# GpSimd held behind each reciprocal root until its normalisation has run, head-group maxima copied as eight rows by two copies, merged comparisons, and another interleaving

## What is computed

```python
x = x + _L0_xattn_ref(_layernorm(x), ctx, ctx, ...)   # 16 heads of 16, softmax
x = x + _L0_ffn_ref(_layernorm(x), gate_w, expert_w)  # x + output of the best of 8 experts
x = x + _L1_xattn_ref(_layernorm(x), ctx, ...)        # 16 heads, scores masked by a fixed pattern
x = x + _L1_ffn_ref(_layernorm(x), ...)               # three cycles of a small gelu net and a twist
x = x + _L2_xattn_ref(_layernorm(x), ctx, ctx, ...)   # linear attention through sigmoids
x = x + _L2_ffn_ref(_layernorm(x), ...)               # linear, plus the best 2 of 8 low-rank experts
x = x + _L3_xattn_ref(_layernorm(x), ctx, ctx, mask, ...)  # one head of 256, softmax
x = x + _L3_ffn_ref(_layernorm(x), ...)               # gated, hidden size 768

def _layernorm(x, axis=-1, eps=1e-05):
    m = jnp.mean(x, axis=axis, keepdims=True)
    v = jnp.var(x, axis=axis, keepdims=True)
    return (x - m) / jnp.sqrt(v + eps)
```

## Time and profile before

| | us |
|---|---|
| three runs | 1043.64, 1046.17, 1047.5 (median 1046.17) |
| profiled execution | 1042.16 |
| its span, first to last instruction | 1040.3 |

### The profile page before, as it was taken

The page is one execution under the profiler, slowest core; times in us unless marked ns, Lnnn a source line. Parts: engine busy times, 40 slices in busy tenths (PEclk is TensorE's granted clock), DMA queues, the critical chain, the costliest instruction groups (busy, mean ns, idle before and its releaser), DMA issues.

```text
span 1040.3 us, 17717 instructions
## 1 busy us (share of the span) xinstructions
PE 973.8 (94%) x6194; PEld 715.1 (69%) x6194; DVE 667.6 (64%) x2250; ACT 561.3 (54%) x1231; POOL 221.8 (21%) x317
## 2 busy tenths in 40 slices
PE   7989889988999999998999999999989999999998
PEld 6765655656577766776587767776577756777777
DVE  5435673577576676777575776774776566746564
ACT  1351645585457653766358643767368543773421
POOL 3004311302240051314030242212221023002210
PEclk9899999999999999999999999999999999999999
DMA  7408525221322031411313211402222004000000
GB/s 234 48 2 237 116 93 111 57 37 32 61 56 62 11 82 32 84 35 35 66 31 68 57 36 26 102 1 55 48 47 51 12 1 101 2 12 1 1 1 21
DMA packets 39927, 56.25 MB, mean 54 GB/s; under 512 B 3968, under 2 KB 35712, under 8 KB 36224
## 3 DMA queue, kind: packets, MB, share of 16 engines
q1 hardware_dynamic: 38448, 46.50, 21.8%
q10 hardware_dynamic: 1392, 8.63, 2.3%
HBM read 39.64 MB, written 13.89 MB: 51 GB/s over the span
## 4 chain that ended last, share of the span: by engine, by line
PE 57%; DVE 16%; ACT 16%; issue 7%; DMA 2%; POOL 2%; SPq 1%; ACTq 0%; DVEq 0%; POOLq 0%
PE bank L1618 7%; PE bank L1945 4%; PE bank L1478 4%; PE bank L1469 4%; PE bank L1675 4%; PE bank L1697 4%; ACT QA L841 4%; PE bank L1956 4%; ACT PT L853 3%; PE bank L1732 3%; PE bank L1590 3%; PE bank L1726 2%; PE bank L1487 2%; ACT L853 2%; PE bank L1678 2%
## 5 line engine op out<-in xcount | busy, mean ns | idle before, releaser
L853 ACT ACTIVATE PT<-bank 128x512 f32<-128x512 f32 x256 | 153.2, 598 | 143.9 <-PE bank L1678 86.6
L1675 PE MATMUL bank<-QA,KA 98*128 98x256 bf16 x512 | 113.2, 273 | 17.2 <-ACT PT L853 15.9
L1618 PE MATMUL bank<-w,xhT 128*128 128x512 f32 x256 | 126.6, 604 | 2.1 <-DVE one L1177 2.1
L1151 DVE CUSTOM_DVE_ANT_0 bank<-bank,maskb 128x256 f32<-128x256 f32 x256 | 102.0, 451 | 26.3 <-PE bank L1590 26.0
L841 ACT COPY QA<-bank 2x256 bf16<-2x256 bf16 x256 | 92.8, 363 | 24.4 <-PE bank L1656 18.4
L1144 DVE TENSOR_REDUCE mx<-bank 128x2 f32<-128x512 f32 x128 | 83.5, 682 | 32.1 <-PE bank L1590 31.4
L1590 PE MATMUL bank<-KA,QA 96*128 96x256 bf16 x512 | 91.0, 274 | 3.2 <-DVE mx L1144 1.4
L1675 PEld LDWEIGHTS bank<-QA,KA 98*128 98x128 bf16 x512 | 46.9, 99 | 64.7 <-issue 43.7
L1945 PE MATMUL bank<-xhBT,wi 128*128 128x256 f32 x336 | 87.6, 391 | 1.4 <-DVE hT L1452 0.6
L1198 DVE SCALAR_TENSOR_TENSOR x<-bank,one,x 128x256 f32<-128x256 f32 x128 | 61.5, 481 | 27.2 <-PE bank L1618 24.7
L1945 PEld LDWEIGHTS bank<-xhBT,wi 128*128 128x128 f32 x336 | 59.6, 192 | 11.5 <-DVE hT L1452 3.2
(11 more groups left out here) (316 smaller groups left out, 2093.1 us busy)
## 6 DMA issues: line engine op xcount, KB each, us to landing
QA<-scratch SPq DMA_DIRECT2D x90, 128.0 KB, 4.4
scratch<-kparts SPq DMA_DIRECT2D x30, 192.0 KB, 2.3
KA<-scratch SPq DMA_DIRECT2D x15, 384.0 KB, 4.6
scratch<-qparts SPq DMA_DIRECT2D x30, 192.0 KB, 2.3
KA<-scratch SPq DMA_DIRECT2D x15, 256.0 KB, 5.4
w<-pack ACTq DMA_DIRECT2D x1, 2409.0 KB, 8.6
wi<-ipack ACTq DMA_DIRECT2D x1, 2304.0 KB, 8.4
xin<-x_in SPq DMA_DIRECT2D x8, 256.0 KB, 5.4
```

Source lines behind the costliest of these rows:

```text
L853: act.activation(PT[:, n % RING, :, :].rearrange("p t s -> p (t s)"), st_bank[:, :], ACT.Exp).then_inc(exp_s, 1)
L1151: last = dve.tensor_tensor_reduce(s, s, maskb[:, t, :], op0=ALU.add, op1=ALU.max, scale=1.0, scalar=-HUGE, accum_out=mx[:, i % 4, n % GH, ...
L1618: last = pe.matmul(bank[n % 2][:, :], xhT[:, kk, t * P:(t + 1) * P], W("exp0", KT)[:, kk, i * 512:(i + 1) * 512], start=(kk == 0), stop=(k ...
L1675: last = pe.matmul(st_bank[:, t * S:(t + 1) * S], KA[m][0:KM, v, t * P:(t + 1) * P], QA[m][0:KM, v, :], start=True, stop=(m == 0))
```

## The change

GpSimd's three root functions end with a wait for the semaphore that VectorE's scaling raises (`xh_s`, or the lane's `xh`), so nothing more runs on GpSimd until that normalisation has run. The maxima of a head group now go to eight adjacent columns of mq, high and low by turns, behind 96 blank ones (MR = 8, KM = 104). The transposed eight rows land on partitions 96 to 103, and every head of the group gets all eight in QA, by one copy for the first head and one for the other three, with the source repeated. KA's eight rows hold ones only in the head's own two: `rows1` makes that pattern from the identity, and `own_rows` spreads it over 16 heads and 256 positions, once for each KA; it waits for the first weights. The second score multiply has 104 rows instead of 98. The pairs of comparisons and of multiplications at L1177, L1358 and L1366 become one `tensor_tensor` each with a repeated second input. The semaphore counts of `negm_s` are adapted. `TURNS` holds the same steps in another order for all five engines, on TensorE with 70 `w` ahead of the first score head, 107 in all, and 64 `z`. On VectorE, `own_rows` stands behind the first sample's scaling and behind its split of the queries (L1064 to 1072), where the two fills had stood first of all. In thread p of the fifth sample (counted from zero), 25 steps of VectorE lie between statistics and scaling in the new order; on GpSimd the split of that sample's keys follows its root.

```diff
--- before.py
+++ after.py
@@ -23,8 +23,9 @@
 
 GROUPS = [(0, 3), (1, 2), (2, 1)]
 KR = PARTS * HD
-KM = KR + 2
-MQ = 32 * (GH - 1) + 2
+MR = 2 * GH
+KM = KR + MR
+MQ = KM
 VW = HD + 1
 E = 8
 R = 4
@@ -87,49 +88,49 @@
...
     "gpsimd":
-        "ppppppssppppsppsssppsppsppasppssspssppaabpppbsbasspbsppaaspppsbppbbsabsppsspppapaspsbbpbsasbsppppspa"
...
+        "ppppppspspppsppssppspppspsasppsspspssappabpbpsbasppbsppsppasasbbpbpsasbsspppppasapbspbpbsabssspppppp"
...
     "tensor":
-        "pwwwppwwwpwwwppwwppwwwwwwwwwwwwwwpwwwwwpwpwwwwwwppwwwwwwwwwwwwwwwwwwwwwwwwwwwsswpsspssvpsvssvsvvswww"
...
+        "pwwwpppwwwppwwwwwwwppwwwwwwwwwwwwwwwwwwwwwwwwwwwwwwpwwwwwpwpwwwwwwppwwwwwwwwwwwwwwwsswpsspssvpssvwsv"
...
@@ -250,6 +251,7 @@
         PT = sb("PT", [P, RING, T, S])
         OT = sb("OT", [P, 2, S])
         rc = sb("rc", [P, T, GH])
+        rows1 = sb("rows1", [KM, GH], BF16)[KR:KM, :]
         att = sb("att", [P, T, D])
         attT = sb("attT", [P, KT, S])
 
@@ -601,11 +603,13 @@
                 pool.wait_ge(stats[t], nth(stats[t], b, n))
                 link(t, pool.tensor_tensor(veps[t][:, :], mv[t][:, :, 1], epsm[:, :], ALU.add))
                 pool.tensor_tensor(rstd[t][:, :], veps[t][:, :], powm[:, :], ALU.pow).then_inc(rstd_s[t], 1)
+                pool.wait_ge(xh_s[t], nth(xh_s[t], b, n))
 
             def norm_part(t, b, n, h, lo, hi):
                 pool.wait_ge(stats[t], of(stats[t], b, n, h))
                 link(t, pool.tensor_tensor(veps[t][:, lo:hi], mv[t][:, lo:hi, 1], epsm[:, lo:hi], ALU.add))
                 pool.tensor_tensor(rstd[t][:, lo:hi], veps[t][:, lo:hi], powm[:, lo:hi], ALU.pow).then_inc(rstd_s[t], 1)
+                pool.wait_ge(xh_s[t], of(xh_s[t], b, n, h))
 
             def split_k(b, m):
                 pool.wait_ge(k_f[m], nth(k_f[m], b, 1))
@@ -684,6 +688,7 @@
                 pool.wait_ge(L.s["stats"], at(L, "stats", b, n, h))
                 link(t, pool.tensor_tensor(veps[t][:, lo:hi], mv[t][:, lo:hi, 1], epsm[:, lo:hi], ALU.add))
                 pool.tensor_tensor(rstd[t][:, lo:hi], veps[t][:, lo:hi], powm[:, lo:hi], ALU.pow).then_inc(L.s["rstd"], 1)
+                pool.wait_ge(L.s["xh"], at(L, "xh", b, n, h))
 
             def rest(L):
                 for b in L.batches:
@@ -837,8 +842,9 @@
                     act.wait_ge(mask_ready, 1)
                 elif q == PLACE[0, 1] and g == 0:
                     act.wait_ge(mask_ready, 2)
-                for h in range(GH):
-                    act.copy(QA[m][KR:KM, g * GH + h, :], ot_b16[32 * h:32 * h + 2, 512:512 + S]).then_inc(negm_s, 1)
+                for lo, hi in ((0, 1), (1, GH)):
+                    act.copy(QA[m][KR:KM, g * GH + lo:g * GH + hi, :],
+                             ot_b16[KR:KM, 512:512 + S].unsqueeze(1).to_broadcast([MR, hi - lo, S])).then_inc(negm_s, 1)
 
             def value():
                 for q in range(len(ATTENTIONS)):
@@ -1159,7 +1165,7 @@
                         top = mx[:, i % 4, :, :].rearrange("p h t -> p t h")
                         if i == 0:
                             dve.wait_ge(pads_ready, 3)
-                        high, low = (mq[:, i % 4, :, c:MQ:32] for c in range(2))
+                        high, low = (mq[:, i % 4, :, KR + c:KM:2] for c in range(2))
                         link("s", dve.tensor_scalar(high, top, -1.0, None, ALU.mult))
                         dve.scalar_tensor_tensor(low, top, -1.0, high, ALU.mult, ALU.subtract).then_inc(mq_s, 1)
                         yield
@@ -1173,9 +1179,8 @@
                                                     ALU.is_equal, ALU.mult)
                 link("s", last)
                 link("s", dve.tensor_reduce(cm2[:, :], c1[:, :, :], AX.X, ALU.max))
-                for t in range(T):
-                    last = dve.tensor_scalar(one[:, t, :], c1[:, t, :], cm2[:, t:t + 1], None, ALU.is_equal)
-                last.then_inc(one_s, 1)
+                dve.tensor_tensor(one[:, :, :], c1[:, :, :], cm2[:, :].unsqueeze(2).to_broadcast([P, T, E]),
+                                  ALU.is_equal).then_inc(one_s, 1)
 
             def experts(b):
                 dve.wait_ge(added, PLACE[b, 0] + 1)
@@ -1221,10 +1226,16 @@
                 dve.tensor_tensor(dst[:, lo:hi, :].rearrange("p t d -> p (t d)"), ps[:, lo * D:hi * D],
                                   src[:, lo:hi, :].rearrange("p t d -> p (t d)"), ALU.add).then_inc(done, 1)
 
+            def own_rows(m):
+                return dve.tensor_copy(KA[m][KR:KM, :, :].rearrange("p (k h) s -> p k h s", h=GH),
+                                       rows1[:, :].unsqueeze(1).unsqueeze(3).to_broadcast([MR, H // GH, GH, S]))
+
             def value():
-                dve.memset(KA[0][KR:KM, :, :], 1.0).then_inc(mask_ready, 1)
-                yield
-                dve.memset(KA[1][KR:KM, :, :], 1.0).then_inc(mask_ready, 1)
+                dve.wait_ge(w_in[0], 16)
+                link("v", dve.tensor_tensor(rows1, ident[KR:KM, KR:KM:2], ident[KR:KM, KR + 1:KM:2], ALU.add))
+                own_rows(0).then_inc(mask_ready, 1)
+                yield
+                own_rows(1).then_inc(mask_ready, 1)
                 yield
                 dve.wait_ge(nomask_in, 16)
                 for t in range(T):
@@ -1354,17 +1365,15 @@
                     link(L.t, last)
                     yield
                     link(L.t, dve.tensor_reduce(L.m2[:, lo:hi], L.r2[:, lo:hi, :], AX.X, ALU.max))
-                    for t in range(lo, hi):
-                        last = dve.tensor_scalar(L.pick2[:, t, :], L.r2[:, t, :], L.m2[:, t:t + 1], None, ALU.is_equal)
-                    link(L.t, last)
+                    link(L.t, dve.tensor_tensor(L.pick2[:, lo:hi, :], L.r2[:, lo:hi, :],
+                                                L.m2[:, lo:hi].unsqueeze(2).to_broadcast([P, hi - lo, E]), ALU.is_equal))
                     link(L.t, dve.scalar_tensor_tensor(L.r3[:, lo:hi, :], L.pick2[:, lo:hi, :], -4.0, L.r3[:, lo:hi, :],
                                                        ALU.mult, ALU.add))
                     yield
                 link(L.t, dve.scalar_tensor_tensor(L.r2[:, lo:hi, :], L.r3[:, lo:hi, :], 0.0, L.r1[:, lo:hi, :],
                                                    ALU.is_lt, ALU.mult))
-                for t in range(lo, hi):
-                    last = dve.tensor_scalar(L.r2[:, t, :], L.r2[:, t, :], L.m1[:, t:t + 1], None, ALU.mult)
-                link(L.t, last)
+                link(L.t, dve.tensor_tensor(L.r2[:, lo:hi, :], L.r2[:, lo:hi, :],
+                                            L.m1[:, lo:hi].unsqueeze(2).to_broadcast([P, hi - lo, E]), ALU.mult))
                 dve.tensor_tensor(L.tw[:, lo:hi, 0:E * R].rearrange("p t (e r) -> p t e r", r=R),
                                   L.sc[:, lo:hi, E:E + E * R].rearrange("p t (e r) -> p t e r", r=R),
                                   L.r2[:, lo:hi, :].unsqueeze(3).to_broadcast([P, hi - lo, E, R]), ALU.mult).then_inc(L.s["rk_dve"], 1)
@@ -1647,7 +1656,7 @@
                 i = q * ITEMS + g
                 pe.wait_ge(mq_s, i + 1)
                 if i:
-                    pe.wait_ge(negm_s, i * GH)
+                    pe.wait_ge(negm_s, 2 * i)
                 if g == 0 and q:
                     pe.wait_ge(added, q)
                 if q:
@@ -1668,7 +1677,7 @@
                         if v < H:
                             n = q * H + v
                             i = n // GH
-                            pe.wait_ge(negm_s, n + 1)
+                            pe.wait_ge(negm_s, 2 * (n // GH) + (1 if n % GH == 0 else 2))
                             if n:
                                 pe.wait_ge(exp_s, n)
                             for t in range(T):
@@ -1703,7 +1712,7 @@
                             pair, half = (v - 10) // (2 * GH), (v - 10) % (2 * GH)
                             i = q * ITEMS + 2 * pair + half
                             pe.wait_ge(ot_s, q * ITEMS // 2 + pair + 1)
-                            pe.wait_ge(negm_s, (q + 1) * H)
+                            pe.wait_ge(negm_s, 2 * (q + 1) * ITEMS)
                             if i:
                                 pe.wait_ge(att_s, i)
                             for t in range(T):
```

70 lines of the change are left out of this document (35 added, 35 removed).

## The result

The changed kernel takes 1004.62 us (median of four runs, 1002.98 to 1006.67) against 1045.64 us for the kernel before in the same comparison: a ratio of 0.961, 95% interval 0.958 to 0.964. It gains 41 us; the prediction said 14 and its range ended at 1017. The direction was right, the size was wrong by a factor of three. The profiled execution took 1002.98 us with a span of 1001.2, 39.1 us less than the 1040.3 before.

What follows compares the result with a forecast made beforehand. TensorE, 94% busy, bound through short hand-overs to VectorE and ScalarE. 12.7 + 8.3 + 1.0 less 3 lost is 19; three quarters, some 14 us, off 1042.16 gives 1028; median 4 higher: 1032 us, range 1017 to 1047.

Steps and rivals of the forecast that it cites:

- last sample: Last sample, run in halves: second half's root starts 0.41 us later in five normalisations; 1 us lost, at most 2.1.
- Part 1: GpSimd held behind each reciprocal root until VectorE's scaling ends: its collisions go, 12.7 us off the chain.
- what would show it: Signs: scalings at 0.41 us everywhere, 128 copies totalling 74 us, first score multiply near 42, TensorE's normalisation waits under half.
- Rival B: Slower, 1057 us, chance 0.10: GpSimd's long hold in lane p delays splits that score heads need, so TensorE stands.
- Part 2: ScalarE's copies of a head group's maxima, two instead of four: 1.16 us instead of 1.45, 8.3 us off the chain.
- rival A: Gain stays off the path, exponential wait untouched, moved GpSimd work hits other VectorE instructions: 1045 us, chance 0.20.
- Part 3: Merged comparisons on VectorE, shortening TensorE's wait for `one`: 1 us gained, bounds 0 and 2.1.
- Part 4, the start: KA's two fills at the start become a later copy of 4.3 us: 2 us lost, bounds 1.3 and 5.
- The discount: Over the whole chain: another queue behind each piece is soon late, so three quarters of 19, some 14 us.
- The order at nothing, plus or minus 5: The new interleaving of the same work on all engines was costed at nothing, plus or minus 5 us.
- C: Everything is returned: 22 us of the chain and a third of VectorE's other 10.6; 1021 us, chance 0.20.

Runs made afterwards that it cites:

- The start partition alone: Kernel before with all four copies of a head group reading at partition 96 (wrong maxima for three heads of four): 1028.47 us, ratio 0.989.

## Why the prediction was wrong in size

What each part gained behind the start, in us. "By the profiles" is from one execution each. "By the whole runs" is from the ratio of the medians, the change of the first score multiply taken off; its intervals are 3 to 4 us to either side.

| part | forecast, by three quarters | alone in the old order, by the profiles | by the whole runs |
|---|---|---|---|
| 1, waits | 9.5 | 10.7 | 10.5 |
| 2, rows and copies | 6.2 | 16.6 | 17.7 |
| 3, comparisons | 0.75 | 4.4 | 2.1 |
| last sample | -0.75 | about 0 | |
| sum of the parts | 15.7 | 31.7 | 30.3 |
| all edits, old order | | 34.4 | 36.1 |
| new order behind the start | 0 | -0.9 | -0.8 |
| start | -1.5 | 5.6 | 5.6 |

34.4 - 0.9 + 5.6 is the 39.1 us of the two spans, where the sum had 14.2. Of the 24.9 us between them part 2 makes 10.4, the start 7.1, part 3 3.7, and what the parts give together beyond their sum 2.7.

**Part 1 held.** Scalings are at 0.41 us everywhere, as "what would show it" asked, and the 12.7 us read off the chain were the right quantity: 10.7 measured. TensorE's waits for scalings fell by 10.3 us in that run, from 16.7 to 6.4. *Rival B's mechanism* exists without its price. In lane p the root leads its scaling by up to 24.8 us, and GpSimd is held all that time. What is behind it is not needed: the key splits' waits on SyncE fell from 313.1 us to 228.0, and TensorE waited for keys once, 5.2 us at 124.92. That wait belongs to the new order, not to the hold: the changed kernel without GpSimd's waits has it too (4.2 us, once), the one with all edits in the old order has none. The *1 us lost in the last sample* did not show: from the last score multiply to the end it is 126.8 us before, 127.4 with the waits alone and 125.6 in the changed kernel.

**Part 2 is the mis-sized term.** The step that failed is "now a head group's maxima take four ScalarE copies of 2x256 at 363 ns, 1.45 us". 363 ns is the duration of one; what a group occupies is the start-to-start time, and 1.52 us for four said so: nearly end to end. Then came "20% less", from a second copy of 0.80 us, measured 787 ns, and a first of 363, measured 365. Both durations were right, but the two overlap, and the group takes 1.06 us, not 1.16. Saved are 0.46 us a group instead of 0.29, on 64 groups 29.6 instead of 18.6 us of ScalarE: a factor of 1.6. The second error is pricing the saving by the copies' 4% of the chain, 8.3 of 18.6 us or 45%, and then by three quarters. The start partition alone frees 22.5 us of ScalarE (64 groups of 1.52 and 1.17) and gave 14.5, 64% of it; all of part 2 frees 29.6 and gave 16.6, 56%. By the whole runs it is 12.4 and 17.7 us, 55 and 60%. So over half of what ScalarE gave up came back, not 45% and not 34%. The exponential queues behind the copies, so what the copies give up is given on to it. That the chain books this under L853 and under multiplies as well as under L841 is a reading that fits; no run shows it by itself. The wait for the exponential was listed and called untouched in rival A; it halved.

**Part 3's step** "I take 1 us, bounds 0 and 2.1" was small but not shown wrong by the merge alone: 4.4 us by the profiles, 2.1 by the whole runs, which is the bound. It failed in the company of part 1. In the old order the hold moves collisions onto this pair (402 to 602 and 638 ns), and there, with the rows as well, the merge is worth 9.2 us (11 by the whole runs, 0.969 against 0.980). In the new order the pair averages 355 ns, and the merge is worth 3.4 behind the start. That a moved collision lands on "other VectorE instructions, as it does on L1177" stood in rival A, as a loss; here the merge caught it in part. The rule that the merged form stays open to collisions held, its mean being 255 ns against 175 undisturbed. Yet it did not make the merge worthless, since one instruction is hit instead of two.

**Part 4, the start.** For the edits in the old order the term held: the first score multiply comes at 44.0 instead of 40.4, 3.6 us late, where 2 had been taken, bounds 1.3 and 5. But the changed kernel has it at 34.8, a gain of 5.6 where "near 42" was expected, because the new order's start was costed at nothing. And "ran before the first normalisation [...], free" failed as a reading. The second fill ended at 10.08 and the first statistics, whose input had long arrived, began right behind it, kernel before:

```profile
10.11 0.75 DVE L1031 BATCH_NORM_STATS2 bst_p<-xin 128x6 f32<-128x256 f32 x2
```

Changed kernel, statistics first, then the two `own_rows`:

```profile
3.65 0.75 DVE L1037 BATCH_NORM_STATS2 bst_p<-xin 128x6 f32<-128x256 f32 x2 [2.20 <-DMA xin<-x_in]
...
8.43 2.29 DVE L1230 COPY KA<-rows 8x4096 bf16<-8x4096 bf16 x1
...
17.77 2.29 DVE L1230 COPY KA<-rows 8x4096 bf16<-8x4096 bf16 x1
```

The two fills had delayed these statistics by 6.5 us and the first scaling by 4.9 (12.39 to 7.47); the weights, which arrive later, hold the rest. The price of the copy failed too: 2.29 us, not 4.3, and less than a fill, which shows as 3.47 with 0.80 of issue ahead of it, so that one fill starts 4.27 behind the other (2.34, 6.61). Still, a plain move of the fills makes the start worse (46.6 against 40.4), for TensorE then idles and runs at 1.2 GHz: the gain needs the move and the re-timed blank multiplies. That "spinning is written into the order" and costs 1.3 us missed this: here the place of the pairs mattered more than their number.

**The discount** of a quarter "since behind each piece stands another queue" was wrong. Alone, the three parts sum to 31.7 us and together give 34.4. Pairs: waits and comparisons 13.9 (sum 15.1), waits and rows 25.2 (sum 27.3). So no part lost a quarter of its worth to another. The likely reason, which no run isolates, is that they shorten different hand-overs of one queue, and that an in-order TensorE that is 94% busy seldom catches up a delay.

**The order at nothing, plus or minus 5,** was right behind the start (0.9 us lost) and wrong as a whole: 34.8 against 44.0 at the start, of which 5.7 us come from TensorE's string alone. It was also no gain of its own: by itself it costs 1.3%.

A slip without consequence: forecast, C and a quarter of A add up to 0.75 for "faster", not 0.76.

*Open:* the last 3.5 us of the start between TensorE's new string alone (38.3) and the whole new order (34.8), where the other engines' strings and the place of the second `own_rows` differ; and the 2.7 us by which the whole exceeds its parts, which is about what the starts of one piece of code differ by (34.8 to 37.7 in three kernels that share order and waits). No run tells these apart. That the waits are worth 23.6 us in the changed kernel and 10.7 in the old one goes mainly with the new order: in the old one they are worth 8.6 with the rows (983.3 to 974.7) and 9.5 with the merges (995.5 to 986.0), in the new order without any edit 14 to 20. Why that order suffers more from collisions is not shown.

## What to carry to other kernels

Price a run of short instructions by the time from start to start, which is read from a timeline, not by their mean duration; and look at what in their operands keeps them apart before merging them. Where the engine that sets the pace is 94% busy and in order, as here, time saved in front of the exponential it waits for most came back by more than half, and savings in different hand-overs added up: do not discount them against each other. Holding the engine that disturbs is worth it if what is queued behind has slack, but look where the disturbance goes next. An order tuned by hand should be run with and without the edits it comes with. Before costing a step at the very start at nothing, check what the engine's next step has been waiting for; and when work ahead of TensorE moves, its fillers must move too.

## What the runs showed of the hardware

Four ScalarE copies of 2x256 out of PSUM with no wait between them take 1.52 us when their source starts at partitions 0, 32, 64 and 96, and 1.17 us when all start at 96, at 361 to 363 ns each, the destination always starting at 96; eight rows behave as two. An 8x768 copy that reads one PSUM row range three times takes 787 ns. On VectorE a broadcast copy of 8x4096 bfloat16 takes 2.29 us, a fill of 2x4096 with a constant 3.47, or 4.27 from one fill's start to the next's. A GpSimd split beside a scaling lengthens VectorE's 0.41 us to as much as 1.25 and takes 1.16 to 1.17 us itself on average with or without. At the start, 3.77 us of idle TensorE were followed by some 10 us at the 1.2 GHz level, 5.77 us by 13.7.
